# An attention product split into three fp32r products, in an adaLN block with bilinear attention and a gated FFN on one core

## The chip, the cores and the metric

One core of a Trainium2 chip runs the whole block. The metric is device time in microseconds (us), the median over the executions; lower is better. Engines by their names in the rows: PE is TensorE's matmul, PEld its weight load, DVE is VectorE, ACT is ScalarE, POOL is GpSimd, SP is SyncE (here it only issues DMAs).

## The reference

Eight batch rows x of 2048 x 256 floats go through two modulated sub-blocks. Cut to what matters:

```python
mod = (silu(c) @ wmod).reshape(8, 6, 1, 256)            # sa, ca, ga, sb, cb, gb
h = layernorm(x) * (1 + ca) + sa
q, k, v = split(h @ w_qkv + b_qkv)                      # 8 heads of 64
scores = einsum('bhld,bhle->bhde', q, k) / 8            # 64 x 64 per head, summed over the 2048 tokens
attn = softmax(scores)
a = layernorm_eps1e6(einsum('bhld,bhde->bhle', v, attn) @ w_fc + b_fc + h) * gamma + beta
x = x + ga * a
h = layernorm(x) * (1 + cb) + sb
xr, xk = (mu * h + (1 - mu) * shifted(h) for mu in (mu_r, mu_k))
x = x + gb * sigmoid(xr @ W_r.T) * (relu(xk @ W_k.T)**2 @ W_v.T)
```

Since the scores are summed over the tokens, everything between the first layernorm `z` and the attention output is linear in `z`. The kernel therefore forms for each batch row the 256 x 256 matrix `z^T z` (gram), from it the scores, the softmax, and one 256 x 256 matrix M that holds v, attention, fc, bias and the residual. The attention output of a token is then `z @ M`.

## The kernel before

The program is written out by hand for five engines, each with its own instruction stream and semaphores between them. A batch row b has 2048 tokens in CH = 4 blocks (j) of 512 tokens; a block has NT = 4 tiles of 128 tokens. `row_steps(b)` on each engine is one step of a software pipeline: it finishes row b (attention product, second layernorm, FFN) and at the same time prepares row n = b + 1 (gram, scores, softmax, M). Row 0 and row B - 2 = 6 have variants of it, rows 1 to 5 are a hardware loop (VectorE) and the last row is `last_row`, where nothing is prepared any more. Before row 0 stands a start part that does the preparation of row 0 and turns the weights.

What the change and the prediction touch:

- **TensorE.** `turn_and_gram(n, j)` (L1260, L1267) turns z of block j into the two banks `tr` and adds to the gram. `attention(b, j)` (L1285) is the product `z_t[:, j] @ m_sb` in plain fp32: 8 matmuls of 256 columns; in the trace a plain fp32 matmul is two records, so a block is x16. `turn_z2` (L1302) turns the second layernorm into the same two `tr` banks. `ffn_r`, `ffn_k` (L1318, L1335) are plain fp32 as well. `ffn_out` (L1151 to L1153, helper `mm3`) is already a product in three parts: operands are split into a high part in fp32r and a low part, and lo*hi, hi*hi and hi*lo are summed; one record each, 24 per block. `wv_attn` (L1389) and `make_m` (L1398) make M of the next row.
- **ScalarE.** `copy_z_t` (L620) takes the turned z out of the `tr` banks; `squares` (L654) sums the squares of the attention output; `take_k` makes relu, square and the high part `k_hi` (L682 to L686).
- **VectorE.** `make_z` (L886), `make_x2` (L896, L901: attention output times 1/std and gate, plus x), `stats_2` (L907 to L917), `mix` (L930, L934), `low_k` (L943: the low part of squared k), `gate_o` (L952), `prep_qk` (L991, L993: the q and k weights of the next row), `take_wvf` (L972 to L977: an fp32 matrix and its high and low part), `softmax_dif`, `softmax_norm`, and `make_m` (L1026: writes `m_sb` from the gram bank and sets `m_ready`).
- **GpSimd.** `rstd_a`, `rstd_2`, `rstd_o` compute the powers -1/2 for three statistics (L453 to L480); `prep_wv` (L496, L499, L506) makes the v weights `wv_aug` of the next row; `fill_x2` (L485) and `add_y` (L512) issue DMAs that add.
- **SyncE.** `next_ca(b)` waits for `m_ready` and `wv_ready` of the row before, then loads the modulation row `rows[:, 3]` (L305), for which VectorE's `prep_now` (L983) waits.

## Time and profile before

| | |
|---|---|
| median of 3 executions | 690.74 us (690.01 to 690.99) |
| the profiled execution | 690.6 us, of which its span is 688.9 us |
| PE busy | 670.7 us, 97% of the span |
| PEld busy | 539.4 us, 78% |
| DVE busy | 561.0 us, 81% |
| ACT busy | 393.8 us, 57% |
| POOL busy | 317.5 us, 46% |
| mean granted TensorE clock | 0.991 of full speed |
| chain that ended last | PE 86%, DVE 7%, POOL 2%, DMA 2% |

The span is the time from the first to the last instruction; 1.7 us of the profiled execution's time lie outside it. Busy shares are of the whole span, so a stage in which one engine never rests is found only in a view by stretches. The chain that ended last is followed back from the last instruction, always to what released it.

### The profile page before, as it was taken

The page shows a single profiled execution, that of the slowest core. Times are in us where ns is not written, and L with a number is a line of the kernel's source. Part 1 is how long each engine was busy: PE and PEld are TensorE (multiplying, and loading weights), DVE is VectorE, ACT ScalarE, POOL GpSimd, SP SyncE. Part 2 cuts the span into 40 slices and gives each one's busy share as a digit, 9 for nine tenths or more (in the row PEclk, how much of TensorE's full clock was granted, in tenths as well). Part 3 has the DMA queues.
Part 4 walks back from the last instruction along what each step waited for, and adds up shares of the span by engine and source line. Part 5 has one row for each costly group of instructions (what it writes and reads, how often), then busy time and mean ns, then how long its engine had stood idle before and what let it go on. Part 6 is the DMA issues. An engine that isn't in the chain of part 4 may idle for free.

```text
span 688.9 us, 11754 instructions
## 1 busy us (share of the span) xinstructions
PE 670.7 (97%) x3712; PEld 539.4 (78%) x3712; DVE 561.0 (81%) x1254; ACT 393.8 (57%) x871; POOL 317.5 (46%) x520
## 2 busy tenths in 40 slices
...
GB/s 316 232 152 222 103 131 123 77 212 97 209 74 142 163 135 147 99 167 92 198 113 79 219 91 213 67 141 158 145 136 99 107 72 173 123 37 179 37 31 91
DMA packets 90984, 93.02 MB, mean 135 GB/s; under 512 B 4224, under 2 KB 89000, under 8 KB 90960
## 3 DMA queue, kind: packets, MB, share of 16 engines
...
q8 instruction: 11, 0.18, 0.1%
q14 instruction: 13, 0.11, 0.0%
...
## 4 chain that ended last, share of the span: by engine, by line
PE 86%; DVE 7%; POOL 2%; DMA 2%; issue 1%; ACT 1%; SPq 0%; DVEq 0%; POOLq 0%
PE work L1335 14%; PE work L1318 14%; PE att L1285 13%; PE gram L1267 11%; PE gram L1398 4%; PE att L1370 4%; PE work L1151 4%; PE tr L1260 4%; PE work L1153 4%; PE work L1152 4%; PE tr L1302 4%; PE att L1389 2%; PE gram L1380 1%; PE att L1318 1%; DVE st L907 1%
## 5 line engine op out<-in xcount | busy, mean ns | idle before, releaser
L471 POOL TENSOR_TENSOR rs<-ve,neg_half 128x4 f32<-128x4 f32 x32 | 41.6, 1300 | 161.4 <-DVE ve L917 161.4
L1285 PE MATMUL att<-m_sb,z_t 128*128 128x256 f32 x496 | 112.4, 380 | 1.6 <-issue 0.8
L1335 PE MATMUL work<-mx,w_k_t 128*128 128x512 f32 x236 | 106.2, 592 | 0.0
L1285 PEld LDWEIGHTS att<-m_sb,z_t 128*128 128x128 f32 x496 | 92.4, 190 | 16.9 <-issue 5.7
L1318 PE MATMUL work<-w_r_t,mx 128*128 128x256 f32 x464 | 105.7, 381 | 0.0
L1318 PEld LDWEIGHTS work<-w_r_t,mx 128*128 128x128 f32 x464 | 85.9, 190 | 11.1
L1267 PE MATMUL gram<-z 128*128 128x256 f32 (+1 forms) x512 | 90.7, 331 | 0.0
L1267 PEld LDWEIGHTS gram<-z 128*128 128x128 f32 x512 | 81.1, 194 | 6.9
L934 DVE SCALAR_TENSOR_TENSOR mx<-t_buf,mu_col,h2t 128x512 f32<-128x512 f32 x120 | 84.3, 765 | 1.1
L654 ACT ACTIVATE sq<-att 128x256 f32<-128x256 f32 x124 | 46.1, 383 | 64.1 <-PE att L1285 64.1
L1335 PEld LDWEIGHTS work<-mx,w_k_t 128*128 128x128 f32 x236 | 44.8, 190 | 44.1 <-issue 42.6
L701 ACT ACTIVATE z<-x,nm,rs 128x256 f32<-128x256 f32 x128 | 66.5, 600 | 21.5 <-POOL nm L473 21.2
L1151 PE MATMUL work<-wvf_lo,k_hi 128*128 128x256 f32 x248 | 75.5, 304 | 1.4 <-issue 1.0
L896 DVE SCALAR_TENSOR_TENSOR t_buf<-att,rs_o,g_row 128x256 f32<-128x256 f32 x124 | 51.4, 477 | 27.8 <-POOL rs_o L480 26.9
L886 DVE TENSOR_SCALAR z<-x_in,ag_a 128x255 f32<-128x255 f32 x128 | 65.1, 570 | 5.1 <-POOL ag_a L465 3.6
L673 ACT ACTIVATE y<-work 128x512 f32<-128x512 f32 x58 | 34.5, 595 | 60.6 <-PE work L1318 60.5
L1153 PE MATMUL work<-wvf_hi,k_lo 128*128 128x256 f32 x248 | 68.9, 278 | 0.0
L1152 PE MATMUL work<-wvf_hi,k_hi 128*128 128x256 f32 x248 | 68.8, 277 | 0.0
L943 DVE TENSOR_TENSOR k_lo<-work,k_hi 128x512 fp32r<-128x512 f32 x61 | 41.2, 688 | 32.0 <-ACT k_hi L686 31.7
L663 ACT ACTIVATE h2t<-tr,mod_now 128x512 f32<-128x512 f32 x64 | 46.3, 778 | 16.0 <-PE tr L1302 16.0
L485 POOL DMA_DIRECT2D x<-in_L_attn_x_dram x32 | 55.2, 1825 | 0.0
L512 POOL DMA_DIRECT2D out_dram<-y x29 | 39.3, 1355 | 34.1 <-DVE y L952 33.7
...
## 6 DMA issues: line engine op xcount, KB each, us to landing
...
```

Source lines behind the costliest of these rows:

```text
L485: nc.gpsimd.dma_start(x2[:, j], x_v[b, j], accum_op=ALU.add).then_inc(x2_filled[j], 16)
L701: ins = nc.scalar.activation(z2[:, t], x2[:, j, t], ACT.Identity, bias=nm_2[:, s, t:t + 1], scale=rs_2[:, s, t:t + 1])
L886: ins = nc.vector.tensor_scalar(z[:, j % 2, t, 0:LAST], x_in[:, j, t, 0:LAST], ag_a[:, j, 3, t:t + 1], ag_a[:, j, 7, t:t + 1], ALU.subtrac ...
L896: ins = nc.vector.scalar_tensor_tensor(t_buf[:, t], att_banks(j, alone)[t // 2][:, (t % 2) * D:(t % 2 + 1) * D], rs_o[:, s, t:t + 1], g_ro ...
L934: ins = nc.vector.scalar_tensor_tensor(dst[:, h], dif[:, h], mu_col[:, n, h:h + 1], prev[:, h], ALU.mult, ALU.add)
L1151: mm(dst, s_hi, m_lo, start=start, stop=False)
L1152: mm(dst, s_hi, m_hi, start=False, stop=False)
L1153: return mm(dst, s_lo, m_hi, start=False, stop=stop)
L1267: ins = mm(gram[:, k * D:(k + 1) * D - k * P], z[:, j % 2, t, k * P:(k + 1) * P], z[:, j % 2, t, k * P:D], start=(j == 0 and t == 0 and k ...
L1285: ins = mm(att_banks(j, alone)[q][:, (t % 2) * D:(t % 2 + 1) * D], z_t[:, j, k, t * P:(t + 1) * P], m_sb[:, k], start=(k == 0), stop=(k == ...
L1318: ins = mm(r_banks(alone)[q][:, (t % 2) * D:(t % 2 + 1) * D], mixed(j, alone)[0][:, ch, tile], w_r_t[:, ch], start=(ch == 0), stop=(ch == ...
L1335: ins = mm(k_banks(alone)[dh][:], w_k_t[:, ch, rows_dh], mixed(j, alone)[1][:, ch], start=(ch == 0), stop=(ch == KD - 1))
```

## The change

The attention product gets the three-part form: `copy_z_hi` writes the turned z as fp32r high part, a new VectorE step `low_z` writes the low part from the same bank, and `make_m` splits M into `m_hi` and `m_lo`; `m_ready` comes with the last of them. `prep_wv` goes from GpSimd to VectorE for rows 1 to 7 (row 0 stays on GpSimd). VectorE's order in `row_steps` is rewritten around these steps. `k_hi` and `k_lo` have one buffer in place of two, and the mixed inputs of the last row's blocks 2 and 3 no longer go into spare z buffers, so `mix` always waits for the products that read its buffer. Where a `tr` bank is filled again, TensorE waits for the low part (`z_lo_ready`) instead of the copy (`z_t_ready`).

```diff
-        z_t = sb("z_t", [P, CH, KD, CT])
+        z_hi, z_lo = (part(n, [P, CH, KD, CT]) for n in ("z_hi", "z_lo"))
+        m_hi, m_lo = (part(n, [P, KD, D]) for n in ("m_hi", "m_lo"))
-        k_hi, k_lo = (part(n, [P, 2, KD, CT]) for n in ("k_hi", "k_lo"))
+        k_hi, k_lo = (part(n, [P, KD, CT]) for n in ("k_hi", "k_lo"))
...
# GpSimd
                 else:
-                    prep_wv(n)
                     rstd_o(b, 1)
...
# ScalarE: copy_z_t -> copy_z_hi, same places
+                    nc.scalar.activation(z_hi[:, j, h], tr[h][:], ACT.Copy).then_inc(z_hi_ready, 1)
...
# VectorE
-            def mix(b, j, made=None, alone=False):
+            def mix(b, j, made=None):
                 i = CH * b + j
-                if not alone:
-                    wait_past(dve, r_done, 2 * i - 2)
-                    wait_past(dve, k_done, 2 * i - 2)
+                wait_past(dve, r_done, 2 * i - 2)
+                wait_past(dve, k_done, 2 * i - 2)
...
+            def low_z(b, j):
+                i = CH * b + j
+                for h in range(KD):
+                    dve.wait_ge(z_hi_ready, 2 * i + h + 1)
+                    nc.vector.tensor_tensor(z_lo[:, j, h], tr[h][:], z_hi[:, j, h].bitcast(F32),
+                                            ALU.subtract).then_inc(z_lo_ready, 1)
...
+            def prep_wv(b):
+                dve.wait_ge(ca_loaded, 16 * (b + 1))
+                wait_past(dve, m_ready, b)
+                nc.vector.tensor_tensor(wv_aug[:], wv_t[:], rows[:, 3].unsqueeze(1).to_broadcast([P, NP, D]),
+                                        ALU.mult).then_inc(wv_step, 1)
+                dve.wait_ge(wv_step, 2 * b + 1)
+                nc.vector.tensor_tensor(wv_aug[:, :, 0:LAST], wv_aug[:, :, 0:LAST],
+                                        wv_aug[:, :, LAST:D].to_broadcast([P, NP, LAST]), ALU.subtract).then_inc(wv_step, 1)
+                dve.wait_ge(wv_step, 2 * b + 2)
+                nc.vector.tensor_copy(wv_aug[:, :, LAST], vb_col[:, :, b]).then_inc(wv_ready, 1)
...
# VectorE, make_m
-                                        res[:].rearrange("p k d -> p (k d)"), ALU.add).then_inc(m_ready, 1)
+                                        res[:].rearrange("p k d -> p (k d)"), ALU.add).then_inc(m_step, 1)
+                dve.wait_ge(m_step, 2 * b + 1)
+                nc.vector.tensor_copy(m_hi[:], m_sb[:]).then_inc(m_step, 1)
+                dve.wait_ge(m_step, 2 * b + 2)
+                nc.vector.tensor_tensor(m_lo[:], m_sb[:], m_hi[:].bitcast(F32), ALU.subtract).then_inc(m_ready, 1)
...
# VectorE, row_steps
                 prep_now(n)
+                low_z(n, 0)
                 make_x2(b, 0)
...
                 else:
+                    make_z(n, 2)
+                    low_k(b - 1, 3)
                     prep_qk(n)
-                    low_k(b - 1, 3)
-                    make_z(n, 2)
+                    low_z(n, 1)
                     make_x2(b, 1)
                     stats_2(b, 1)
                 mix(b, 0)
+                low_z(n, 2)
...
                 mix(b, 1)
+                low_z(n, 3)
                 gate_o(b, 0)
                 make_x2(b, 3)
                 mix(b, 2)
                 low_k(b, 1)
+                prep_wv(n)
                 stats_2(b, 3)
-                if far:
-                    stats_a(n + 1, 0)
                 gate_o(b, 1)
                 softmax_dif(n)
                 if far:
-                    stats_a(n + 1, 1)
+                    stats_a(n + 1, 0)
                 softmax_norm(n)
                 if far:
+                    stats_a(n + 1, 1)
                     make_z(n + 1, 0)
+                    stats_a(n + 1, 2)
                     make_z(n + 1, 1)
-                    stats_a(n + 1, 2)
                 low_k(b, 2)
                 make_m(n)
...
# TensorE, attention
-                            ins = mm(att_banks(j, alone)[q][:, (t % 2) * D:(t % 2 + 1) * D], z_t[:, j, k, t * P:(t + 1) * P], m_sb[:, k],
-                                     start=(k == 0), stop=(k == KD - 1))
+                            ins = mm3(att_banks(j, alone)[q][:, (t % 2) * D:(t % 2 + 1) * D],
+                                      (z_hi[:, j, k, tile], z_lo[:, j, k, tile], m_hi[:, k], m_lo[:, k]),
+                                      start=(k == 0), stop=(k == KD - 1))
```

VectorE's stream at the beginning of a row in the loop, between the statistics of block 0 (`ve`) and the attention output of block 1 (`t_buf`), before:

```order
L917 TENSOR_SCALAR ve<-ag 128x4
L991 SCALAR_TENSOR_TENSOR wqk_aug<-wqkv_sb,d_now,wqk_aug 128x1024 [waits prep_base]
...
L943 TENSOR_TENSOR k_lo<-work,k_hi 128x512 [waits k_hi_ready]
...
L886 TENSOR_SCALAR z<-x_in,ag_a 128x255 [waits z_used]
L886 TENSOR_SCALAR z<-x_in,ag_a 128x255 x3
L894 REGISTER_ALU [waits xk_mixed]
L896 SCALAR_TENSOR_TENSOR t_buf<-att,rs_o,g_row 128x256 [waits rs_o_ready]
```

The same place in the changed kernel (`wqk_aug` are the q and k weights, `k_lo` the low part of squared k, `z_lo` the new low part):

```order
L911 TENSOR_SCALAR ve<-ag 128x4
L875 REGISTER_ALU
L878 REGISTER_ALU [waits rs_a_ready]
L880 TENSOR_SCALAR z<-x_in,ag_a 128x255 [waits z_used]
L880 TENSOR_SCALAR z<-x_in,ag_a 128x255 x3
L942 ISA
L944 TENSOR_TENSOR k_lo<-work,k_hi 128x512 [waits k_hi_ready]
...
L992 SCALAR_TENSOR_TENSOR wqk_aug<-wqkv_sb,d_now,wqk_aug 128x1024 [waits prep_base]
...
L936 TENSOR_TENSOR z_lo<-tr,z_hi 128x512 [waits z_hi_ready]
```

The q and k weights now stand behind the low part of squared k, z of block 2 ahead of it, and a low part of z between them and the attention output.

A second place on VectorE, later in the loop, behind the mixed inputs (`mx`) of block 2; `st` are the statistics of block 3. Before:

```order
L934 SCALAR_TENSOR_TENSOR mx<-t_buf,mu_col,h2t 128x512 x3
L941 REGISTER_ALU
L943 TENSOR_TENSOR k_lo<-work,k_hi 128x512 [waits k_hi_ready] x2
L907 BN_STATS st<-x 128x6 [waits x2_ready]
L907 BN_STATS st<-x 128x6 x3
```

And in the changed kernel, with the v weights (`wv_aug`) between the two:

```order
L927 SCALAR_TENSOR_TENSOR mx<-t_buf,mu_col,h2t 128x512 x3
L942 REGISTER_ALU
L944 TENSOR_TENSOR k_lo<-work,k_hi 128x512 [waits k_hi_ready] x2
L1002 TENSOR_TENSOR wv_aug<-wv_t,rows 128x1024 [waits m_ready,ca_loaded]
L1004 ISA
L1005 TENSOR_TENSOR wv_aug<-wv_aug 128x4x255 [waits wv_step]
L1007 REGISTER_ALU
L1008 REGISTER_ALU [waits wv_step]
L1008 COPY wv_aug<-vb_col 128x4
L901 BN_STATS st<-x 128x6 [waits x2_ready]
```

Everything that follows on VectorE up to M of the next row (output gate, softmax, z of the row after, `k_lo` of block 2) stands behind these three instructions.

## Rows read from the trace of the kernel before

**Rows 1.** The page: busy time, share of the span and instructions.
```profile
PE 670.7 (97%) x3712; PEld 539.4 (78%) x3712; DVE 561.0 (81%) x1254; ACT 393.8 (57%) x871; POOL 317.5 (46%) x520
```
**Rows 2.** Busy time by stretch: rows 0, 2, 6 and the last one.
```profile
core 0: us, PE busy (x) PEld busy (x) DVE busy (x) ACT busy (x) POOL busy (x), PEclk, DMA share, GB/s
57.20:128.50 71.30, 68.89 (x379) 55.46 (x380) 61.62 (x146) 44.21 (x100) 41.50 (x68) 1.00 0.57 137
208.70:289.00 80.30, 80.26 (x452) 65.14 (x451) 68.62 (x152) 48.69 (x108) 38.53 (x64) 1.00 0.62 137
529.60:609.80 80.20, 80.17 (x452) 65.06 (x451) 61.56 (x132) 48.61 (x108) 31.98 (x36) 1.00 0.56 115
609.80:688.90 79.10, 69.77 (x360) 54.48 (x359) 57.16 (x119) 42.46 (x96) 22.68 (x23) 0.99 0.41 74
```
**Rows 3.** TensorE's timeline in row 3: start us, us, engine, line, operation, xcount.
```profile
309.26 0.28 PE L1152 MATMUL work<-wvf_hi,k_hi 128*128 128x256 f32 x1
...
311.87 1.03 PE L1260 MATMUL tr<-ident,z 128*128 128x128 f32 x8
...
316.24 3.62 PE L1285 MATMUL att<-m_sb,z_t 128*128 128x256 f32 x16
319.69 1.04 PE L1260 MATMUL tr<-ident,z 128*128 128x128 f32 x8
```
**Rows 4.** Groups by line and shape: busy us, mean ns | idle before, releaser.
```profile
L943 DVE TENSOR_TENSOR k_lo<-work,k_hi 128x512 fp32r<-128x512 f32 x61 | 41.2, 688 | 32.0 <-ACT k_hi L686 31.7
L975 DVE CAST wvf_hi<-t_buf 128x512 fp32r<-128x512 f32 x7 | 3.3, 476 | 0.2
L977 DVE TENSOR_TENSOR wvf_lo<-t_buf,wvf_hi 128x512 fp32r<-128x512 f32 x7 | 4.8, 692 | 0.2
L901 DVE TENSOR_TENSOR x<-t_buf,x 128x1024 f32<-128x1024 f32 x32 | 39.2, 1225 | 1.1
L496 POOL TENSOR_TENSOR wv_aug<-wv_t,rows 128x1024 f32<-128x1024 f32 x8 | 20.8, 2596 | 11.8 <-DVE mx L859 11.8
L1153 PEld LDWEIGHTS work<-wvf_hi,k_lo 128*128 128x128 f32 x248 | 46.6, 188 | 0.0
```
**Rows 5.** VectorE's timeline in row 2, with its idle time in brackets.
```profile
213.41 1.40 DVE L876 BATCH_NORM_STATS2 st_a<-x_in 128x6 f32<-128x256 f32 x4
...
219.21 1.66 DVE L896 SCALAR_TENSOR_TENSOR t_buf<-att,rs_o,g_row 128x256 f32<-128x256 f32 x4 [2.48 <-POOL rs_o L480]
...
227.50 1.28 DVE L943 TENSOR_TENSOR k_lo<-work,k_hi 128x512 fp32r<-128x512 f32 x2
228.70 3.89 DVE L886 TENSOR_SCALAR z<-x_in,ag_a 128x255 f32<-128x255 f32 x4
...
242.92 1.28 DVE L952 SCALAR_TENSOR_TENSOR y<-y,work 128x512 f32<-128x512 f32 x2
...
253.31 1.37 DVE L886 TENSOR_SCALAR z<-x_in,ag_a 128x255 f32<-128x255 f32 x4
```
**Rows 6.** TensorE's and ScalarE's timelines in row 2.
```profile
211.34 3.62 PE L1285 MATMUL att<-m_sb,z_t 128*128 128x256 f32 x16
...
243.00 3.62 PE L1318 MATMUL work<-w_r_t,mx 128*128 128x256 f32 x16
...
232.32 1.08 ACT L620 ACTIVATE z_t<-tr 128x512 f32<-128x512 f32 x2 [1.52 <-PE tr L1260]
```
**Rows 7.** The start part in the timelines of GpSimd, TensorE and VectorE.
```profile
48.66 0.31 POOL L506 COPY wv_aug<-vb_col 128x4 f32<-128x4 f32 x1
...
49.88 2.80 PE L1389 MATMUL att<-wv_aug,attn 128*128 128x256 f32 x8
...
57.19 0.69 DVE L1026 TENSOR_TENSOR m_sb<-gram,res 128x512 f32<-128x512 f32 x1 [5.48 <-PE gram L1398]
...
63.81 0.15 DVE L983 TENSOR_SCALAR neg_d<-rows 128x1 f32<-128x1 f32 x1 [5.66 <-DMA rows<-row_scratch]
```
**Rows 8.** Line 305, the load of the modulation row: issue to landing over its 8 transfers.
```profile
DMA to landing us min/median/max: 2.9/3.0/5.8
```

More of the change, by code:

```diff
@@ L162, in y_buf, with k_split, mixed @@
             return x_in[:, j] if alone else y[:, j % 2]
-        def k_split(j):
-            return k_hi[:, j % 2], k_lo[:, j % 2]
+        def k_split(j, alone):
+            return (z_hi[:, 0], z_hi[:, 1]) if alone and j == CH - 1 else (k_hi, k_lo)
         def o_banks(j, alone):
             return att if alone and j == CH - 1 else work[0:2]
-        def mixed(j, alone):
-            return (z_t[:, 2 * j - CH], z_t[:, 2 * j - CH + 1]) if alone and j >= CH // 2 else (xr[:, j % 2], xk[:, j % 2])
+        def mixed(j):
+            return xr[:, j % 2], xk[:, j % 2]
         wmod_sb = h2t[:, :, 1:1 + 6 * D]
@@ L537, in row_steps @@
                 rstd_o(b, 3)
-                if first:
-                    prep_wv(n)
                 add_y(b, 0)
@@ L931, in mix @@
                 dve.wait_ge(dif_done, i + 1)
-                for n, (dst, ready) in enumerate(zip(mixed(j, alone), (xr_mixed, xk_mixed))):
+                for n, (dst, ready) in enumerate(zip(mixed(j), (xr_mixed, xk_mixed))):
                     for h in range(KD):
@@ L941, in low_k @@
                     dve.wait_ge(k_hi_ready, 2 * i + h + 1)
-                    hi, lo = k_split(j)
+                    hi, lo = k_split(j, alone)
                     nc.vector.tensor_tensor(lo[:, h], k_banks(alone)[h][:], hi[:, h].bitcast(F32), ALU.subtract).then_inc(k_lo_ready, 1)
@@ L1097, in last_row @@
                 stats_2(b, 3)
-                mix(b, 2, alone=True)
+                mix(b, 2)
                 gate_o(b, 0)
                 low_k(b, 1, alone=True)
-                mix(b, 3, alone=True)
+                mix(b, 3)
                 gate_o(b, 1, alone=True)
@@ L1249, in turn_and_gram @@
                 pe.wait_ge(z_ready, i + 1)
-                if first or j == 1:
-                    wait_past(pe, z_t_ready, 2 * i)
-                elif j == 0:
+                if j == 0:
                     wait_past(pe, h2_ready, 2 * CH * (b - 1))
-                else:
+                elif not first and j > 1:
                     pe.wait_ge(h2_ready, 2 * (CH * (b - 1) + j - 1))
                 for h in range(KD):
+                    if j > 0 and (first or j == 1):
+                        pe.wait_ge(z_lo_ready, 2 * i - 1 + h)
                     for t in range(NT):
```

70 lines of the change are left out of this document (37 added, 33 removed).

## The prediction

> **What bounds the kernel now.** I began with the busy times. Of the span of 688.9 us TensorE is busy 97% and VectorE 81% [rows 1], so both are near their end. Second, the view by stretches, cut where `m_sb` is written, once a row [rows 2]. In a row of the loop (80.3 us) TensorE rests 0.04 us and VectorE is busy 68.6 us; row 6, which prepares no statistics, has VectorE at 61.6; in the last row TensorE is busy only 69.8 of 79.1 us. The reader is to see that TensorE alone sets the loop, and that VectorE has 11.7 us a row to give away before it sets it too. Third, the timelines of a row, for who waits when.
>
> **The attention product.** A block of it occupies TensorE for 319.69 - 316.24 = 3.45 us [rows 3]. The product of three parts with the same shapes is there already: 23 products in 311.87 - 309.26 = 2.61 us, 0.1135 us each, so 24 take 2.73 [rows 3]. A block saves 0.72 us, a row 2.9, all 32 blocks 23.1 us. Bounds: the shapes are those of the row, so only the step from fp32 to fp32r before each block is open, at most about 0.1 us a block (3 us in all). If TensorE stayed the only bound, this would be the result, nearly.
>
> **What VectorE gets, a row.** A low part of z is the form of L943 (0.69 us, PSUM and SBUF in, fp32r out) [rows 4]; two back to back take 228.70 - 227.50 = 1.20 us of the stream [rows 5]. Four pairs: 4.8 us. M's split: a cast and a subtraction as in L975 and L977, 0.48 + 0.69 us, about 1.2 [rows 4]. The v weights: two 128x1024 operations as L901, 1.23 each, and a copy of four columns: 2.7 us. Its nearest rows set the bounds: 2.45 (two L901 alone) and 5.2 (twice GpSimd's 2.60) [rows 4]; I take the VectorE row, since it is the same engine and size. Given back: z of block 2 took 3.89 us while GpSimd made the v weights, and 1.37 with GpSimd quiet [rows 5], so 2.5 us return. The rule of the Trainium skill, page "SBUF — State Buffer", section "Who interferes with whom", is that VectorE and GpSimd hold a shared port pair exclusively and the later one blocks; by that rule, the trace agrees (3.89 against 1.37). Sum: 4.8 + 1.2 + 2.7 - 2.5 = 6.2 us a row.
>
> **The two engines side by side.** TensorE: 80.3 - 2.9 = 77.4 us a row. VectorE: from the 80.3 I take its waits over 0.3 us (nine in row 2, 10.0 together, the largest 2.48 [rows 5]); 70 us of work and short hand-overs remain, plus 6.2 is 76.2. They are 1 us apart, so each wait between them counts on one or the other. I laid one row out on both, with time 0 at the first attention block (211.34 [rows 6]) and durations of the trace; positions below are mine.
>
> Where VectorE still waits:
> - The attention output of block 0 needs `rs_o`, which GpSimd computes behind the statistics that end the row's first stretch: 219.21 - 214.73 (start 213.41 plus 1.32) = 4.5 us [rows 5]. In it VectorE now has a gate (1.2), small copies (0.8) and the first low part (1.2): 1.3 left.
> - The low part of block 1 follows TensorE's FFN output (2.73), which follows `k_lo`, then the turn and the copy (the copy starts 0.63 after the turn and its first half takes 0.6 [rows 6], hand-overs 0.2): 4.2 us, in which VectorE has only the q and k weights, 3.2. Left: 1.0.
> - `k_lo` of block 1 waits for ScalarE, as all `k_lo` do (32 us in 61 [rows 4]): 1.0.
> - z for the row after waits for GpSimd's statistics: 0.7.
>
> Together 4.0, so 76.2 + 4.0 = 80.2.
>
> Where TensorE now waits: 0.4 for `k_lo` of the previous row's block 3 (0.3 before; its cover was two fp32 attention blocks, 1.4 us longer, but the q and k weights, 3.2 us, no longer stand ahead of it); 1.45 at the second half of `ffn_r` of block 0, whose bank needs the first half of the output gate. That gate started at 242.92 and `ffn_r` at 243.00 [rows 5, 6], so its second half (1.73 later) had 1.1 us of slack; three shorter attention blocks bring TensorE 2.2 us forward, while the gate, now behind three low parts and M's split, comes no earlier (0.2 us later). And 1.3 at `ffn_out` of block 2: from `k_lo` of block 1 on, VectorE has 18.8 us up to `k_lo` of block 2, the v weights among them, TensorE 17. Together 77.0 + 3.15 = 80.1. The two sums agree; I take 80.1 for rows 1 to 5, against 80.2 on average before: **-0.5 us in five rows**. 2.9 us saved on TensorE, almost all of it turned into waits for VectorE.
>
> M's split itself is covered in the loop: `ffn_out` of block 2 (2.73) runs while VectorE needs 0.46 + 1.9 from TensorE's last M product. Were that cover gone it would cost 1.2 a row.
>
> **Row 6** has 7 us less on VectorE, so the last stall falls away: 77.0 + 0.4 + 1.45 = 78.9, -1.3 us. **Last row**: laid out in the same way, -1.6 us of the possible 2.9, the rest lost in its chain of normalizations; the single k buffer and the waits added to `mix` cost 0, since the products that they wait for are over 5 us old.
>
> **Start and row 0** are where it costs. Of row 0's four low parts two fall into waits of VectorE; the other two stand ahead of the statistics of row 1's first blocks, 2 x 1.2 = 2.4 us. GpSimd finishes the v weights of row 0 behind those statistics, at 48.97 (start 48.66), and TensorE takes them at 49.88 [rows 7]: slack 0.8, so 1.6 late. M's split is uncovered here (VectorE had waited 5.48 us, nothing else runs [rows 7]): +1.2. So `m_ready` comes 2.8 later. The modulation row is loaded only after it, and VectorE waited 5.66 us for that, until 63.81 [rows 7]. That transfer took 5.8 where the median is 3.0 [rows 8], behind GpSimd's four filling DMAs, which start 2.5 later now. So the wait ends between 63.8 (issue 60.7 plus 3.0) and 66.6 (plus 5.8); I take 66.2, as the queue moves along. The low part of block 0 makes it +3.5 for the attention output. From there VectorE never rests in this row (61.6 busy of 71.3, and the first 6 us idle [rows 2, 7]): two more low parts, +2.4, and hand-overs +0.2 to `ffn_out` of block 0, then the stall at block 2's `k_lo`, +1.0: **+7.1 us at the end of row 0**, the shorter attention blocks included. Bounds: +4.3 (landing at 63.8) to +7.9.
>
> **Sum:** 7.1 - 0.5 - 1.3 - 1.6 = +3.7 on the profiled 690.6, 694.3. The median of the runs is 0.14 above that execution: 694.4.
>
> **Rivals.**
> 1. *VectorE stays ahead; TensorE alone bounds.* For it: 76.2 is below 77.4. Against: the four waits above are chains through ScalarE and GpSimd, not slack. -2.9 in each of seven rows and the last, + 5 at the start: 690.7 - 23.1 + 5 = 672.6. Chance 0.04.
> 2. *The other side: the hand-over to the output gate is looser.* Place: second half of `ffn_r`, block 0. If VectorE's path to the gate is 1 us a row shorter than my layout (the waits for `rs_o` and for the low part of block 1 add 2.3 us to it, and both are differences of long chains), a row is 79.1 and five take 5.0 off: 689.4; with 1.5 us, 686.9. It decides from 0.75 us a row on (3.7 over five rows), where the loop has won what the start lost. Against: both chains are read from timelines with errors of a few tenths. Chance 0.18.
> 3. *VectorE is dearer than laid out:* a further wait per row, such as GpSimd's small operations held up or low parts late for the `tr` banks. 1.2 us a row: 700.4. Chance 0.12.
> 4. *The split product is not faster, because weight loads bind it:* 24 loads of 0.188 us are 4.5 us a block [rows 4], 1.06 over the fp32 block: 690.7 + 34 + 5 = 730. The FFN block with the same 24 loads runs in 2.73 us [rows 3], so chance 0.01. The Trainium skill, page "Perfetto Trace Analysis", section "Identifying the Most-Contended Engine", takes the share of weight loading for a good measure of how near TensorE is to its bound; by that measure this block would be over it, and row and rule differ.
>
> A price by a page: the Trainium skill, page "FP8 and Floating Point Precision", section "TensorE Precision Notes", counts four passes for true fp32; three against four would make a block 2.59 us, an estimate from that page and the 3.45, and 4.5 us more would be saved on TensorE in all; the row decides, 2.73.
>
> **How the numbers follow.** A measurement of this kernel can tell about 0.2%, 1.4 us, from no change. My forecast, waits nearly as laid out, has 0.65; it spreads some 3 us either way and lies mostly above +1.4, with 0.15 within 1.4 us, 0.47 above, 0.03 below. Rivals 1 and 2 are faster (0.22, of which 0.02 falls within), rivals 3 and 4 slower (0.13). Faster 0.23, same 0.17, slower 0.60. The range runs from 687.0 (rival 2 with 1.5 us a row) to 700.5 (rival 3), and leaves out rival 1 and the ends.
>
> **What would show it.** Right: `att` matmuls of 0.11 us spacing; VectorE busy 74 to 76 us in a loop row, TensorE idle about 3 us there, before `ffn_r` (released by the output gate) and `ffn_out` (released by `k_lo`); M of row 0 written 1.6 later, the modulation row in row 0 waited for until about 66. Wrong: loop rows of 77 to 78 us (rival 1), `z` of block 2 still above 2 us, or a stall at a place not named here, such as the turns into `tr`.

## The result: 5 us slower, and the profile after

The changed kernel takes 695.72 us (median of 4 runs, 694.19 to 697.01) against 690.75: ratio 1.0069, 95% interval 1.0057 to 1.0082. The forecast was 694.4 with a range of 687.0 to 700.5 and the larger chance on slower. The profiled execution is the fastest of the four (694.19, span 692.6), 3.6 us above that of before, so the remaining 1.4 us to the medians are not in the trace read here. TensorE's mean granted clock was 0.994 in this execution and 0.985 to 0.989 in the other three, which took 1.0 to 2.8 us longer; the clock is taken up below the table of the experiments.

The page's busy times of the changed kernel:

```profile
PE 655.0 (95%) x3968; PEld 535.2 (77%) x3968; DVE 605.8 (87%) x1355; ACT 391.3 (56%) x871; POOL 277.5 (40%) x499
```

Against [rows 1] TensorE has lost 15.7 us of work and VectorE has gained 44.8. The view by stretches, cut at the writing of `m_sb` as in [rows 2]: row 0, a row of the loop, row 6, the last row.

```profile
core 0: us, PE busy (x) PEld busy (x) DVE busy (x) ACT busy (x) POOL busy (x), PEclk, DMA share, GB/s
56.00:131.80 75.80, 66.96 (x410) 54.80 (x409) 67.72 (x158) 44.11 (x100) 29.63 (x61) 1.00 0.50 122
293.09:373.80 80.71, 78.37 (x481) 64.59 (x481) 74.38 (x166) 48.28 (x108) 33.35 (x61) 1.00 0.61 136
535.19:614.60 79.41, 78.45 (x483) 64.88 (x484) 67.03 (x146) 48.27 (x108) 29.06 (x38) 1.00 0.61 123
614.60:692.60 78.00, 67.74 (x392) 54.14 (x390) 58.40 (x121) 42.29 (x96) 23.05 (x23) 0.99 0.41 75
```

By the times at which `m_sb` is written, `m_sb` of row 1 comes 3.3 us later than before (131.82 against 128.48), rows 1 to 5 take 80.67 on average against 80.25 (+2.1), row 6 0.7 less and the last row 1.1 less: 3.3 + 2.1 - 0.7 - 1.1 = 3.6.

TensorE in the row that starts at 293.09. The two entries of idle time are the second half of `ffn_r` of block 0, released by the output gate, and `ffn_out` of block 2 (read as "issue", since the wait is on its weight load; `k_lo` was written just before). The first line is M's last product, in front of it. The `att` rows are the first and the last product of an attention block.

```profile
288.17 3.70 PE L1426 MATMUL gram<-wfc_c,gq 128*128 128x256 f32 x16
293.27 0.36 PE L1177 MATMUL work<-wvf_lo,k_hi 128*128 128x256 f32 x1 [1.41 <-issue]
...
296.18 0.28 PE L1177 MATMUL att<-m_lo,z_hi 128*128 128x256 f32 x1
...
298.93 0.28 PE L1179 MATMUL att<-m_hi,z_lo 128*128 128x256 f32 x1
...
328.84 1.99 PE L1346 MATMUL work<-w_r_t,mx 128*128 128x256 f32 x8 [0.92 <-DVE y L953]
```

The same place in the kernel before:

```profile
285.26 3.70 PE L1398 MATMUL gram<-wfc_c,gq 128*128 128x256 f32 x16
288.61 0.47 PE L1151 MATMUL work<-wvf_lo,k_hi 128*128 128x256 f32 x1
```

From start to start this is 5.1 us against 3.35, so the stall before `ffn_out` of block 2 costs 1.77 us in each of rows 1 to 5; the bracket says 1.41 because it counts from the modelled end of the record before, and that lies 0.35 us behind the start of the next product in the kernel before (285.26 + 3.70 against 288.61). `ffn_r` of block 0 takes 4.64 us from start to start against 3.46: its stall costs 1.19, where the bracket says 0.92. The two together are 2.96 us a row, and the split product gives back 2.4.

VectorE in the same row, where it waits or is stretched:

```profile
293.09 0.68 DVE L1039 TENSOR_TENSOR m_sb<-gram,res 128x512 f32<-128x512 f32 x1
...
304.58 1.66 DVE L890 SCALAR_TENSOR_TENSOR t_buf<-att,rs_o,g_row 128x256 f32<-128x256 f32 x4 [1.22 <-POOL rs_o L483]
...
309.73 1.38 DVE L880 TENSOR_SCALAR z<-x_in,ag_a 128x255 f32<-128x255 f32 x4
...
316.56 1.29 DVE L936 TENSOR_TENSOR z_lo<-tr,z_hi 128x512 fp32r<-128x512 f32 x2 [1.07 <-ACT z_hi L614]
...
328.11 1.28 DVE L953 SCALAR_TENSOR_TENSOR y<-y,work 128x512 f32<-128x512 f32 x2
...
354.00 0.69 DVE L944 TENSOR_TENSOR k_lo<-work,k_hi 128x512 fp32r<-128x512 f32 x1 [1.04 <-ACT k_hi L680]
354.61 1.22 DVE L1002 TENSOR_TENSOR wv_aug<-wv_t,rows 128x1024 f32<-128x1024 f32 x1
355.86 1.22 DVE L1005 TENSOR_TENSOR wv_aug<-wv_aug 128x1020 f32<-128x1020 f32 x1
...
367.25 1.37 DVE L880 TENSOR_SCALAR z<-x_in,ag_a 128x255 f32<-128x255 f32 x4 [0.66 <-POOL ag_a L468]
...
370.36 2.21 DVE L880 TENSOR_SCALAR z<-x_in,ag_a 128x255 f32<-128x255 f32 x4 [0.42 <-POOL ag_a L468]
372.60 1.29 DVE L944 TENSOR_TENSOR k_lo<-work,k_hi 128x512 fp32r<-128x512 f32 x2
```

The four waits of the hand-made layout are all there, at their places and nearly at their sizes (1.22, 1.07, 1.04, 0.66 against 1.3, 1.0, 1.0, 0.7). In the start and row 0 (`m_sb` of row 0 and the operation behind the modulation row, against 57.19 and 63.81 [rows 7]):

```profile
56.04 0.69 DVE L1039 TENSOR_TENSOR m_sb<-gram,res 128x512 f32<-128x512 f32 x1 [4.93 <-PE gram L1426]
...
62.80 0.15 DVE L984 TENSOR_SCALAR neg_d<-rows 128x1 f32<-128x1 f32 x1 [4.60 <-DMA rows<-row_scratch]
```

### The profile page after: what moved, and what is told of

Read it like the earlier page. It is cut to its first block and busy times, and to the rows that moved or that the text cites. A ratio compares the mean times of both kernels' runs of the same rounds, so it can differ in the third digit from the quotient of the medians.

```text
span 692.6 us, 12399 instructions
## 1 busy us (share of the span) xinstructions
PE 655.0 (95%) x3968; PEld 535.2 (77%) x3968; DVE 605.8 (87%) x1355; ACT 391.3 (56%) x871; POOL 277.5 (40%) x499
## 5 line engine op out<-in xcount | busy, mean ns | idle before, releaser
L1346 PE MATMUL work<-w_r_t,mx 128*128 128x256 f32 x464 | 107.5, 382 | 5.4 <-DVE y L953 5.4
L474 POOL TENSOR_TENSOR rs<-ve,neg_half 128x4 f32<-128x4 f32 x32 | 37.2, 1164 | 183.0 <-DVE ve L911 183.0
L1363 PE MATMUL work<-mx,w_k_t 128*128 128x512 f32 x244 | 109.9, 592 | 0.0
L1293 PE MATMUL gram<-z 128*128 128x256 f32 (+1 forms) x512 | 89.1, 327 | 0.0
L927 DVE SCALAR_TENSOR_TENSOR mx<-t_buf,mu_col,h2t 128x512 f32<-128x512 f32 x128 | 87.7, 748 | 1.1
L1177 PE MATMUL att<-m_lo,z_hi 128*128 128x256 f32 x248 | 74.2, 299 | 4.5 <-DVE t_buf L890 2.5
L1178 PE MATMUL att<-m_hi,z_hi 128*128 128x256 f32 x248 | 70.0, 282 | 0.0
L1179 PE MATMUL att<-m_hi,z_lo 128*128 128x256 f32 x248 | 70.0, 282 | 0.0
L890 DVE SCALAR_TENSOR_TENSOR t_buf<-att,rs_o,g_row 128x256 f32<-128x256 f32 x124 | 51.3, 477 | 10.4 <-POOL rs_o L483 9.6
L1177 PEld LDWEIGHTS work<-wvf_lo,k_hi 128*128 128x128 f32 x248 | 46.6, 188 | 17.4 <-issue 16.4
L880 DVE TENSOR_SCALAR z<-x_in,ag_a 128x255 f32<-128x255 f32 x128 | 50.0, 453 | 7.4 <-POOL ag_a L468 6.4
```

What stands on the lines that cost most here:

```text
L880: ins = nc.vector.tensor_scalar(z[:, j % 2, t, 0:LAST], x_in[:, j, t, 0:LAST], ag_a[:, j, 3, t:t + 1], ag_a[:, j, 7, t:t + 1], ALU.subtrac ...
L890: ins = nc.vector.scalar_tensor_tensor(t_buf[:, t], att_banks(j, alone)[t // 2][:, (t % 2) * D:(t % 2 + 1) * D], rs_o[:, s, t:t + 1], g_ro ...
L927: ins = nc.vector.scalar_tensor_tensor(dst[:, h], dif[:, h], mu_col[:, n, h:h + 1], prev[:, h], ALU.mult, ALU.add)
L1177: mm(dst, s_hi, m_lo, start=start, stop=False)
L1178: mm(dst, s_hi, m_hi, start=False, stop=False)
L1179: return mm(dst, s_lo, m_hi, start=False, stop=stop)
```

## The experiments

In the expectations T is the account that is tested, and R, S, P and the other rivals are what would hold if it were wrong (in e8 the account is called G). All ratios are to the kernel before, run beside (690.7 to 691.4 us); a difference between two experiments is the difference of their ratios times 690.8. "Row" is the distance between two writings of `m_sb`, in the loop (the mean of rows 1 to 5, which differ by at most 0.6, in e6 and e9 by 1.3) and in row 0.

| kernel | us | ratio (95%) | row of the loop | row 0 | half clock in the start / row 0, us |
|---|---|---|---|---|---|
| before | 690.75 | | 80.25 | 71.3 | 10.2 / 0 |
| changed | 695.72 | 1.0069 (1.0057-1.0082) | 80.67 | 75.8 | 6.8 / 0 |
| e1_fp32 | 707.34 | 1.0230 (1.0211-1.0249) | 82.3 | 76.1 | 10.2 / 0 |
| e2_no_low | 685.60 | 0.9918 (0.9903-0.9933) | 79.4 | 73.7 | 10.2 / 0 |
| e3_wv_pool | 705.79 | 1.0206 (1.0187-1.0225) | 81.5 | 79.7 | 10.2 / 3.4 |
| e4_order | 700.60 | 1.0132 (1.0115-1.0149) | 81.1 | 79.0 | 10.2 / 6.8 |
| e5_low_z_behind_gate | 696.74 | 1.0081 (1.0068-1.0094) | 80.9 | 75.7 | 10.2 / 0 |
| e6_z_on_scalar | 697.30 | 1.0083 (1.0068-1.0098) | 79.9 | 77.8 | 20.5 / 3.4 |
| e7_before_wv | 696.22 | 1.0075 (1.0062-1.0087) | 81.1 | 71.7 | 13.7 / 0 |
| e8_wv_ahead | 700.68 | 1.0130 (1.0114-1.0147) | 80.9 | 77.4 | 13.7 / 3.4 |
| e9_both | 692.96 | 1.0027 (1.0013-1.0040) | 79.7 | 80.5 | 13.7 / 10.2 |
| e10_before_z_scalar | 694.97 | 1.0050 (1.0034-1.0066) | 80.1 | 74.6 | 10.2 / 0 |
| e11_ordered | 683.45 | 0.9899 (0.9881-0.9917) | 78.4 | 74.4 | 10.2 / 0 |

The last column is of the profiled execution. For a few us at a time TensorE was granted the lower of its two levels, 1.2 GHz and not 2.4 (PEclk 0.50). No row of the loop has such a stretch in any trace, so the loop's column is free of it, while the start and row 0 are not. In the kernel before the first stretch lies at 14.2; at the same time the changed kernel ran at 1.00:

```profile
14.20:17.60 3.40, 3.40 (x13) 2.95 (x11) 2.54 (x8) 1.08 (x2) 2.26 (x9) 0.50 1.04 408
```
```profile
14.20:17.60 3.40, 3.40 (x25) 3.07 (x23) 2.97 (x9) 1.09 (x2) 2.22 (x9) 1.00 1.03 410
```

The first gram of z, most of it in this stretch, took 4.37 us in the kernel before and 2.78 in the changed one:

```profile
14.34 4.37 PE L1267 MATMUL gram<-z 128*128 128x256 f32 x16
```
```profile
14.81 2.78 PE L1293 MATMUL gram<-z 128*128 128x256 f32 x16
```

So part of what the "row 0" column and the time of `m_sb` of row 0 show is the clock of that one execution. The profiled execution of e9 is also the slowest of its twelve (695.72, median 692.96).

**e1_fp32: the product undone, the rest kept.**

```diff
-ins = mm3(att_banks(...), (z_hi[...], z_lo[...], m_hi[:, k], m_lo[:, k]), ...)
+ins = mm(att_banks(...), z_hi[:, j, k, tile].bitcast(F32), m_sb[:, k], ...)
```

> The attention product goes back to one fp32 product (m_sb by z_hi, four passes); the split of M and the low parts of z are still made, but not multiplied, so the low part of z is missing from the output. It prices what VectorE got, with the old TensorE. Theory T (the gain of the split product is real, about 2.4 us a row on TensorE, and VectorE's in-order stream takes it back): a row of the loop is 80.3 + the stalls for k_lo (up to 1.4) and none for the gate, 81 to 82.5 us, the whole 698 to 706. Rival S (the split product gives nothing, since both kernels' rows are set by VectorE and its waits alone): a row stays at 80.7 and the whole at 695 to 697.

Measured: 707.34, row 82.3; 1.3 over T's range, far from S. (A stall of 0.6 at the gate, which T had put at nothing, is in the row: `ffn_r` takes 4.07 from start to start.) So the change is two halves: VectorE's new work costs 2.30% or 15.9 us, and the split product gives back 1.61% or 11.1.

**e2_no_low: low parts of z left out after row 0.**

```diff
+n = CT if full else 4
-nc.vector.tensor_tensor(z_lo[:, j, h], tr[h][:], z_hi[:, j, h].bitcast(F32), ...)
+nc.vector.tensor_tensor(z_lo[:, j, h, 0:n], tr[h][:, 0:n], z_hi[:, j, h, 0:n].bitcast(F32), ...)
```

> The low part of z is made in full for row 0 only; for rows 1 to 7 only 4 of 512 columns of each half are renewed, so the output lacks most of the low part there. It takes 4.4 us a row from VectorE and leaves every wait and every product. T: VectorE's path falls to about 76.3, TensorE's 77.8 plus 0.3 to 1 of waits sets the row: 78 to 79 us instead of 80.7, the whole 678 to 685. Rival R (TensorE with its slower pace of 0.1195 us a product and the chains through ScalarE set the row, VectorE's work does not): 80.3 to 80.7, the whole 693 to 696.

Measured: 685.60, 1.51% or 10.4 us below the changed kernel; T, though 0.6 over its range. The row is 79.4, not 78 to 79, because only the stall before `ffn_r` went. The one before `ffn_out` of block 2 stayed as it was (5.1 us from start to start, 1.77 of it stall): from `k_lo` of block 1 to `k_lo` of block 2 VectorE takes 18.6 us (348.90 to 367.49 here, 354.00 to 372.60 above), no low part of z lies between, and the v weights do.

**e3_wv_pool: the v weights back on GpSimd.**

```diff
 low_k(b, 1)          # VectorE
-prep_wv(n)
 stats_2(b, 3)
...
 else:                # GpSimd
+    prep_wv(n)
+    bias_wv(n)
     rstd_o(b, 1)
```

> Only the making of the v weights of rows 1 to 7 goes back to GpSimd, where the kernel before has it. T, as in the prediction (2.7 us of work against 2.5 us of stretched z): the stall before ffn_out of block 2 (1.4) shrinks, but z of block 2, stretched by 2.5 again, stands ahead of the output gate, and the stall before ffn_r grows from 0.9 to about 3: a row of 81 to 82, the whole 697 to 705. Rival (the move cost 2.7 and gave nothing back): the whole 680 to 690, a row of 78.5 to 79.5.

**e7_before_wv: that move alone, in the kernel before.** The same lines, the other way round, in the kernel before.

> The kernel before, and only the v weights of rows 1 to 7 moved from GpSimd to VectorE, at the place where the changed kernel has them (fp32 product, old order of the q and k weights). T: though VectorE is busy only 68.6 of 80.2 us here, it has 15 us between k_lo of block 1 and that of block 2 and gets 2.7 more, so TensorE waits about 1.2 at ffn_out of block 2; the z that is no longer stretched gives nothing back, since its time lies beside TensorE: a row of 81 to 81.7, the whole 696 to 701. Rival (VectorE's idle time absorbs it, as its busy share says): 80.2 a row, 690 to 692.

Measured: e3 705.79 (0.8 over the range given), row 81.5; e7 696.22, row 81.1. Of the times both are nearer to T than to its rival. The row of the loop in e7, and the second half of the VectorE stretch in it:

```profile
292.71:373.83 81.12, 80.56 (x449) 65.06 (x449) 68.45 (x156) 48.38 (x108) 34.28 (x61) 1.00 0.61 136
```
```profile
354.63 0.69 DVE L940 TENSOR_TENSOR k_lo<-work,k_hi 128x512 fp32r<-128x512 f32 x1 [1.04 <-ACT k_hi L683]
355.23 1.22 DVE L998 TENSOR_TENSOR wv_aug<-wv_t,rows 128x1024 f32<-128x1024 f32 x1
...
372.63 1.29 DVE L940 TENSOR_TENSOR k_lo<-work,k_hi 128x512 fp32r<-128x512 f32 x2
373.83 0.68 DVE L1035 TENSOR_TENSOR m_sb<-gram,res 128x512 f32<-128x512 f32 x1
```

In e7 VectorE is busy no longer than before (68.45 of 81.12; the 2.7 us and the stretched z cancel, z of block 2 takes 1.37 again), and yet the row is 0.8 longer: the added work stands in the stretch that ends at `ffn_out` of block 2, which now comes 0.80 later behind M's last product (4.15 us from start to start for 3.35). The returned time lies where nobody waited for it: VectorE's wait for `rs_o` behind z is 2.51 instead of 1.18.

In e3 the size came out and the place did not. z of block 2 is not stretched, because in the changed order it is done before GpSimd begins the v weights. What is stretched is what VectorE does beside them, the first half of the q and k weights and of `res`, 4.75 us instead of 1.76:

```profile
316.46 1.38 DVE L887 TENSOR_SCALAR z<-x_in,ag_a 128x255 f32<-128x255 f32 x4
...
318.96 2.65 DVE L999 SCALAR_TENSOR_TENSOR wqk_aug<-wqkv_sb,d_now,wqk_aug 128x1024 f32<-128x1024 f32 x1
321.54 2.10 DVE L1001 SCALAR_TENSOR_TENSOR res<-last_c,neg_d,res 128x256 f32<-128x256 f32 x1
```
```profile
318.13 2.40 POOL L497 TENSOR_TENSOR wv_aug<-wv_t,rows 128x1024 f32<-128x1024 f32 x1
320.61 2.75 POOL L500 TENSOR_TENSOR wv_aug<-wv_aug 128x1020 f32<-128x1020 f32 x1
```

And the stall before `ffn_r` did not grow to 3, it stayed at 1.2. TensorE lost 1.9 us around the turn of z2, ahead of the attention product of block 2, which waits for the attention output of block 1:

```profile
328.15 0.36 PE L1183 MATMUL att<-m_lo,z_hi 128*128 128x256 f32 x1 [1.00 <-DVE t_buf L897]
```

It got 1.1 back before `ffn_out` of block 2. The move costs 5.2 us (0.75%) with the fp32 product in the old order and gains 9.5 (1.37%) in the changed kernel, because there the work that GpSimd's v weights stretch stands in the stretch up to the output gate, which is short of time.

**e4_order and e8_wv_ahead: the v weights in VectorE's waits.**

```diff
 low_z(n, 0)
+prep_wv(n)           # first operation, 1.22 us
 make_x2(b, 0)        # waits 1.22 for rs_o
...
 prep_qk(n)
+centre_wv(n)         # second operation and copy
 low_z(n, 1)
...
-low_z(n, 2)          # e4_order alone: behind the gate
 gate_o(b - 1, 3)
+low_z(n, 2)
```

> The same work in another order on VectorE: the first v weights operation (1.22) stands before the attention output of block 0, where VectorE waits 1.22 for rs_o; the second and the copy stand before the low part of block 1, where it waits 1.07; and the low part of block 2 stands behind the output gate. T: about 2.3 us of VectorE's waits are filled, the stall before ffn_out of block 2 (1.4) goes, and that before ffn_r (0.9) too: a row of 78 to 78.8, the whole 678 to 685. Rival R (waits on VectorE are incidental): within 2 us of the changed kernel, 694 to 697.

> Of the reordered kernel e4_order only the part with the v weights: first operation ahead of the attention output of block 0 (in the wait for rs_o), second and copy ahead of the low part of block 1; the low part of block 2 stays ahead of the output gate. Theory G, formed from e4_order: the wait for rs_o is no free time, because GpSimd is held up while VectorE runs that operation, so rs_o comes 0.9 later; the gate comes 1.5 to 2.5 later than in the changed kernel, the stall before ffn_r grows to 2.5 to 3.5, that before ffn_out of block 2 goes: a row of 81.3 to 82.3, the whole 700 to 706. Rival (e4_order lost its time only by moving the low part behind the gate, which stalls the attention product of block 3): 79 to 80.5, the whole 683 to 694.

Measured: e4 700.60, where 678 to 685 was expected: this expectation failed, and R failed too. The wait was filled and did not go: VectorE still waits 0.90 for `rs_o`. GpSimd's operation that makes it, in the changed kernel and in e4:

```profile
303.54 1.01 POOL L483 TENSOR_TENSOR rs_o<-ve_o,neg_half 128x4 f32<-128x4 f32 x1
```
```profile
308.20 1.86 POOL L483 TENSOR_TENSOR rs_o<-ve_o,neg_half 128x4 f32<-128x4 f32 x1
```
```profile
307.93 1.26 DVE L1002 TENSOR_TENSOR wv_aug<-wv_t,rows 128x1024 f32<-128x1024 f32 x1
310.09 1.66 DVE L890 SCALAR_TENSOR_TENSOR t_buf<-att,rs_o,g_row 128x256 f32<-128x256 f32 x4 [0.90 <-POOL rs_o L483]
```

1.01 us became 1.86 beside VectorE's 128x1024 operation. And the place that the v weights left had hidden 1.3 us of waits for TensorE (the gate of block 1 and the maximum of the scores), which now show. So the stall before `ffn_out` of block 2 shrank by 1.1 us and did not go. In its place, in both kernels, `ffn_out` of block 3 comes 1.0 later (its `k_lo` stands behind the later attention output) and the turn of z2 0.4 later. In e4 the stall before `ffn_r` went, but 1.4 us came before `ffn_out` of block 0, as in e5 below.

e8 has the same 1.86 and the same 0.90, so G's first half, `rs_o` 0.9 later, held. Its second half did not: the stall before `ffn_r` stayed at 1.2 where G had 2.5 to 3.5, and the row is 80.9 against 81.3 to 82.3. The total, 4.2 us over the changed kernel by the ratios, is at the lower edge of G's range, and 1.2 of it come from row 6 and some 1.6 from row 0, with which G had not reckoned. (In the trace `m_sb` of row 1 comes 4.6 us later than in the changed kernel; 3.0 of these are the start, where the code is the same and TensorE ran 7 us more at the lower clock, and row 0 has 3.4 more at it.)

**e5_low_z_behind_gate.** The last hunk above alone.

> The changed kernel, and only the low part of block 2 moved from ahead of the output gate of the row before's block 3 to behind it, in rows 1 to 6. T: the gate comes 1.2 us earlier, so the stall before ffn_r (0.9 to 1.2) goes; of VectorE's wait at k_lo of block 1 (1.04) nothing is left, and the stall before ffn_out of block 2 (1.4) stays: a row of 79.6 to 80.2, the whole 688 to 693. Rival (the order does not matter, VectorE's total work sets the row): 80.7, 694 to 697.

Measured: 696.74, row 80.9; the rival. The stall before `ffn_r` is gone, and it is back later in the row, before `ffn_out` of block 0, which waits for `k_lo` of block 0 behind the moved low part:

```profile
339.23 0.36 PE L1178 MATMUL work<-wvf_lo,k_hi 128*128 128x256 f32 x1 [1.24 <-issue]
```

So over this stretch VectorE's work counts as a sum, and its order only chooses the place of the wait.

**e6_z_on_scalar: take work off VectorE instead.** z of the coming rows by four ScalarE activations a block (2.07 us), GpSimd makes the bias.

```diff
+act.wait_ge(rs_a_ready, i + 1)
+for t in range(NT):
+    ins = nc.scalar.activation(z[:, j % 2, t, 0:LAST], x_in[:, j, t, 0:LAST], ACT.Identity,
+                               bias=ag_a[:, j, 0, t:t + 1], scale=ag_a[:, j, 7, t:t + 1])
```

> The changed kernel with z of rows 1 to 7 (but for the two blocks made in the start) normalized by ScalarE, with a bias of -mean times rstd (one more small operation on GpSimd a block), at four places where ScalarE is idle for 2.4 to 6.6 us. It takes 6.4 us a row from VectorE, 3.6 of them between k_lo of block 1 and k_lo of block 2, 1.4 ahead of the output gate. T: both of TensorE's stalls go, the row is TensorE's own 77.8 to 78.5, the whole 674 to 682, faster than both kernels. Rival P (product pace and chains through ScalarE set the row, and more on ScalarE delays its copies): 80 to 82, the whole 690 to 705.

Measured: 697.30, in P's range and not in T's. The row fell only to 79.9. In the trace the start took 6.0 us more than in the changed kernel and row 0 2.0 more, with TensorE at the lower clock for 17 us more in the two together; how much of the 8 us is the clock and how much the added GpSimd operation was not separated. VectorE had time now (68.6 busy of 80.1) and the stall before `ffn_out` of block 2 was gone, but 1.2 stayed before `ffn_r` and 1.0 came at the turn of z2 of block 0: VectorE waits for ScalarE there, which waited for GpSimd.

```profile
318.96 2.08 ACT L697 ACTIVATE z<-x,nm,rs 128x256 f32<-128x256 f32 x4 [2.10 <-POOL nm L478]
```
```profile
323.00 1.29 DVE L956 TENSOR_TENSOR z_lo<-tr,z_hi 128x512 fp32r<-128x512 f32 x2 [2.14 <-ACT z_hi L616]
```

**e9_both and e10_before_z_scalar.** e9 is e6 with the low part of block 2 behind the gate and the statistics of block 3 earlier; e10 gives the kernel before the same z on ScalarE.

> e6_z_on_scalar with three edits: the low part of block 2 behind the output gate as in e5_low_z_behind_gate; the statistics of the row after's block 3 ahead of k_lo of block 2, where VectorE waited 1.8 for ScalarE; and GpSimd's extra operation left out for the six blocks of the start. In e6 the row was 80.1, with a stall of 1.2 at ffn_r and one of 1.0 at the turn of z2 of block 0, which came through GpSimd's statistics ahead of rs_o; t_buf of block 2 no longer has z of VectorE ahead of it, so e5's stall at the attention product of block 3 should not come. T: a row of 78 to 78.8, start and row 0 as in the changed kernel, the whole 680 to 686. Rival P (a stall moves again, to a place not yet seen): 79.5 to 80.2, the whole 688 to 696.

> The kernel before, with z on ScalarE in the same way and the same place of the statistics, fp32 product and v weights on GpSimd left. VectorE gets 8 us a row of idle time more, but TensorE, busy the whole 80.2, sets the row. T: 80.0 to 80.4 a row, the whole 689 to 693. Rival (the gain in e9_both would come from z on ScalarE alone, not from the split product together with it): the whole 680 to 686 here too.

(The stall that these expectations place at the attention product of block 3 was misread: the entry above shows it before `ffn_out` of block 0.) Measured: e9 692.96, rows of 79.2 and 80.4 in turn, P and not T; e10 694.97, 2 us over T's range, with rows of 80.1 as T says but a row 0 of 74.6 instead of 71.3, which T had left out. In e9's row 0 ScalarE, in order, waited 9.13 us for GpSimd's statistics before it could do anything else, and TensorE 5.21 for ScalarE. The clock was at its lower level from 94.6 to 101.4, so the second half of the product took 3.78 us, where the first had taken 1.88:

```profile
93.05 2.07 ACT L710 ACTIVATE z<-x_in,ag_a 128x255 f32<-128x255 f32 x4 [9.13 <-POOL ag_a L473]
```
```profile
88.56 1.88 PE L1381 MATMUL work<-mx,w_k_t 128*128 128x512 f32 x4
95.65 3.78 PE L1381 MATMUL work<-mx,w_k_t 128*128 128x512 f32 x4 [5.21 <-ACT y L672]
```

In every second row GpSimd did the statistics of the coming blocks beside VectorE's split of M and mix. The records of its first small operations, which overlap each other, are up to 2.67 us long, 13 times the usual 0.20, and `rs_o` was queued behind them:

```profile
218.60 2.67 POOL L458 TENSOR_TENSOR ag_a<-st_a 128x4 f32<-128x4 f32 x1
```
```profile
230.41 1.66 DVE L913 SCALAR_TENSOR_TENSOR t_buf<-att,rs_o,g_row 128x256 f32<-128x256 f32 x4 [2.91 <-POOL rs_o L488]
```

**e11_ordered: these three places mended.**

```diff
 make_x2(b, 2)        # VectorE
+low_k(b, 0)
 stats_2(b, 2)
-low_k(b, 0)
...
 rstd_o(b, 0)         # GpSimd, rows after the first
+rstd_a(n, 2)
...
 rstd_2(b, 0)
+rstd_a(n, 3)
...
-rstd_a(n + 1, 2)     # was at the end of the row
-rstd_a(n + 1, 3)
```

and `make_z(1, 2)`, `make_z(1, 3)` on VectorE in row 0.

> e9_both with three places mended that its trace shows: k_lo of block 0 ahead of the statistics of block 2 (in e9_both, as in e5_low_z_behind_gate, the stall that left ffn_r came back before ffn_out of block 0, 1.1 to 1.4 us, behind k_lo); GpSimd's statistics of the row after's blocks 2 and 3 behind rs_o of block 0 instead of ahead of it (its small operations took 0.6 to 2.7 us beside VectorE's mix, rs_o came up to 1.7 later and every second row lost 1.1 more); z of row 1's blocks 2 and 3 made by VectorE in row 0 (there e9_both's TensorE stood still for 7 us). T: a row of 77.9 to 78.6, row 0 75 to 77, the whole 679 to 684. Rival P: a stall appears elsewhere, rows of 79 to 80, the whole 686 to 692.

Measured: 683.45, ratio to before 0.9899 (0.9881 to 0.9917): 7.0 us faster than before and 1.7% or 11.7 us faster than the changed kernel. The start and row 0 have the clock stretches of before, and the two spans differ by 7.0 us as well (681.9 against 688.9). The total is in T's range; the loop as T says, row 0 a little under its 75 to 77:

```profile
57.10:131.50 74.40, 67.05 (x411) 55.06 (x412) 65.41 (x154) 44.56 (x102) 29.69 (x58) 1.00 0.48 122
288.26:366.64 78.38, 78.15 (x483) 64.68 (x483) 68.73 (x150) 56.27 (x125) 34.21 (x65) 1.00 0.63 141
```

TensorE rests 0.2 of 78.4 us: it sets the row again, 1.9 us shorter than before. e10, with the fp32 product, stays at 80.1 (TensorE busy 80.08 of 80.08), so z on ScalarE alone does not give this, and the changed kernel, e4, e5 and e8 show that the split product in four orders on VectorE does not either. How much each of the three mended places brings, and whether some order would do without z on ScalarE, was not tried.

## Why the prediction was right, and where its terms were off

The time, the sign and the mechanism held: the product's gain is taken back by VectorE's one stream (e1, e2), at the two stalls named, `ffn_r` of block 0 behind the gate and `ffn_out` of block 2 behind `k_lo`. But that the total is so near to the forecast is luck, because two errors cancel in the profiled execution: the loop was forecast too good by 2.6 us in rows 1 to 5, 0.6 in row 6 and 0.5 in the last, the start with row 0 too bad by 3.8. Nor are the 3.8 all the forecast's: e5 has the changed kernel's code in the start and row 0 and the clock stretches of before, and its `m_sb` of row 1 is 4.15 us later than before, not 3.3:

```profile
132.63 0.68 DVE L1039 TENSOR_TENSOR m_sb<-gram,res 128x512 f32<-128x512 f32 x1
```

So of the 3.8 about 0.8 goes with the clock of one execution, and 2.95 are the forecast's. The medians are 5.0 apart where the forecast had 3.7: by them it was 1.3 too low.

- **The attention product.** "24 take 2.73" was mis-sized. An `att` block takes 298.93 - 296.18 = 2.75 us for 23 spacings, 0.1195 each, 2.87 for 24, in every block; with what follows, a row gets 2.4 us instead of 2.9. The nearest row of the trace had the same shapes and other buffers. The 0.1 us that the prediction had left open for the step between forms (at most 0.1 a block) is about this size, but it comes from the pace within the block. Why it is 0.1195 and not 0.1135 was not tried and stays open.
- **VectorE's work.** Low parts 1.20 a pair (1.29 by the trace's entry, overlapping), v weights 2.7, M's split 1.2, z of block 2 at 1.38 instead of 3.89: as priced. The Trainium skill, page "SBUF — State Buffer", section "Who interferes with whom", stood behind the returned 2.5 us, and the trace agrees (1.38 against 3.89). It works the other way too, and there the prediction did not use it: e4's `rs_o` at 1.86 instead of 1.01. And e3 shows that the 2.5 us at z hang on the old order: in the new one GpSimd's v weights stretch the q and k weights, by 3.0 us.
- **The two sides.** Forecast 80.1, measured 80.67. VectorE's waits are 4.4 instead of 4.0 (0.42 at the second z of the row after was left out). On TensorE 0.5 comes from the product's pace; the stalls cost 1.77 and 1.19, together 2.96, for 1.3 and 1.45, together 2.75, and of the 0.4 at block 3's `k_lo` only 0.1 came. The sum of both works out: 80.25 - 2.43 + 2.96 = 80.78 for a row of 80.7. The prediction itself takes 77.4 us for TensorE's own work in one place and 77.0 in the sum, and of the 0.4 between them it names only the 0.3 of before at block 3's `k_lo`.
- **M's split** is covered in the loop: no wait of TensorE at the first attention block of a row, right.
- **Row 6** was 79.4, not 78.9, and the **last row** gave 1.1, not 1.6: the same mis-sized product, 0.56 us a row by the pace, is an estimate for most of it. The single k buffer and the waits added to `mix` cost nothing that can be seen: in the last row VectorE's waits for `k_hi` of the first blocks are 1.40, 1.04, 0.82 and 1.04 us, before 1.41, 1.04, 0.84 and 1.04, and no `mix` waits for TensorE.
- **Start and row 0** is the step that failed, in its first half. "Two low parts ahead of the statistics, 2.4 us, so the v weights 1.6 late": these statistics started at 41.1 to 41.3 in the three kernels with the old start (before, e7, e10) and at 40.8 to 42.0 in six of the seven with the new one and nothing else changed in it (43.6 in e8), some 0.5 us later and not 2.4. Part of the two low parts went into VectorE's waits for x (2.85 us at 19.59 before, at most 0.9 there in all seven), and another 1.2 came back at the mean of the output weights (last section). `m_sb` of row 0 can be compared where the clock stretches are the same, 3.4 and 6.8 us: it was written at 57.2 and 57.3 with the old start (before, e10) and at 56.7 to 57.2 with the new one (e1 to e5, e11). So it comes up to 0.6 us earlier, and the forecast delay of 1.6 did not come. With more time at the lower clock it is later whatever the start (58.4, 59.0 and 59.0 in e9, e7 and e8 with 13.7 us of it), and the 56.0 of the changed kernel goes with 6.8 us of it. M's split cost its 1.2, so the modulation row was issued at 57.95, not 60.7 (before: 57.91), and was waited for until 62.8, not 66.2: 4.9 us from issue to use, where the forecast had 5.5 and the kernel before 5.9. From there on the step was right: `m_sb` of row 1 follows 69.0 us later, 4.35 more than before; the forecast had 4.7. The bounds of the step do not follow from its terms: a landing at 63.8 or 66.6 gives +4.7 or +7.5, not +4.3 and +7.9.
- **The rivals.** Rival 1 was excluded by e1 and e2; rival 4 by the pace, since weight loads of 0.19 us overlap at a spacing of 0.12. Rival 2, a looser hand-over to the gate, did not occur: the gate starts 31.9 us after the row's first attention block, 0.35 more than before, forecast 0.2 more. Its price of 1 us a row was sound: with the low parts left out of the path to the gate (e2) the stall of 1.19 there goes and the row is 1.2 shorter. Order alone does not do this (e5): with the gate 1.2 us earlier for TensorE the wait comes back at `ffn_out` of block 0.

## What to carry to other kernels

When work moves to an engine, do not ask whether it has idle time but which stretch between two of its hand-overs gets the work: 2.7 us into the short stretch cost 0.8 us a row although the engine's busy time did not change (e7). A stall that was removed by order alone came back at a later hand-over (e4, e5); the faster product counted only when work was taken off the stretch (e2, e11). Before filling a wait, look at who is working during it: if it is GpSimd, and the filler is a large VectorE operation on SBUF, most of the wait may come back behind the filler (0.90 of 1.22 us in e4). And before comparing two traces in a start part, compare the granted clock there.

## What the runs showed of the chip

- GpSimd's small operations (128x4, usually 0.20 us) took up to 2.67 us, in overlapping records, beside VectorE operations of 128x1024 and 128x512 in e9, and its power operation 1.86 instead of 1.01 in e4. I had known this for the large v weights only [rows 4, 5].
- The same three-part product has more than one pace at the full clock: 0.1195 us for the attention product in every block, 0.1136 or about 0.118 for the FFN's in one and the same execution.
- It works the other way on small operations too: the mean of the output weights (VectorE, 128x4) took 1.34 us in all three kernels with the old start, where it began at 37.0 to 37.2 beside GpSimd's making of the v weights (in the kernel before that operation ran from 36.17 to 38.51, and the mean ended at 38.54), and 0.17 in all ten with the new one, where it begins 0.13 us before the other's end (37.81 and 37.94 in the changed kernel). The added low parts moved it there and so got 1.2 us back.
- TensorE's granted clock fell to its lower level in row 0 of five of the thirteen profiled executions (e3, e4, e6, e8, e9), each time during or within 0.9 us after a rest of TensorE of 2.5 to 5.2 us (in e9 also once after one of 2.0, which the traces of e1, e2 and e5 have as well without a fall). In the rows of the loop it never fell.
